# Four transformer layers on one core: unit loads, weight loads and padding memsets moved across the border between a layer's prologue and its attention

## What is computed

```
x = x + linear_attention(xn)    * silu(moe_ffn(xn))        # layer 0
x = x + relative_attention(xn)  * silu(ternary_ffn(xn))    # layer 1
x = x + rotary_attention(xn)    * silu(grouped_ffn(xn))    # layer 2
x = x + biased_attention(xn)    * silu(clamped_ffn(xn))    # layer 3
```

## Time and profile before

| | |
|---|---|
| median of 3 runs | 2297.72 us (2287.29 to 2298.31) |
| the profiled execution | 2273.22 us, span 2271.4 us, mean granted clock 0.867 |
| PE busy | 1774.4 us (78%) |
| DVE busy | 1304.1 us (57%) |
| ACT busy | 916.0 us (40%) |
| POOL busy | 413.6 us (18%) |
| PE idle before its first matmul of a causal attention | 32.0 us (layer 2), 36.2 us (layer 3) |

### The profile page before, as it was taken

One profiled execution on the slowest core, in us unless ns is written; L12 is line 12 of the kernel. 1 busy time (PEld: TensorE's weight loads), 2 busy tenths in 40 slices (PEclk: granted clock), 3 DMA queues, 4 the chain that ended last, 5 costly groups with the idle time before them and its releaser, 6 DMA issues. The chain is left out here.

```text
span 2271.4 us, 33714 instructions
## 1 busy us (share of the span) xinstructions
PE 1774.4 (78%) x12423; PEld 817.5 (36%) x12423; DVE 1304.1 (57%) x2569; ACT 916.0 (40%) x1719; POOL 413.6 (18%) x340
## 2 busy tenths in 40 slices
PE   5895999537888888888463898885973998969998
PEld 4633444313343333333232343342431444333333
DVE  3224444648466766582433987515464977327888
ACT  1111222414565666566232366651220666532221
POOL 0000000266466756562003000000001000000000
PEclk7787999758999999899786799987985999779999
DMA  4100000356567666562005001000024011000000
GB/s 127 44 19 1 0 0 0 108 160 168 138 147 176 154 160 163 143 168 59 10 23 156 12 21 30 16 1 0 0 65 124 17 30 30 2 1 1 0 0 19
DMA packets 190782, 141.38 MB, mean 62 GB/s; under 512 B 56697, under 2 KB 169513, under 8 KB 190506
## 3 DMA queue, kind: packets, MB, share of 16 engines
q1 hardware_dynamic: 184010, 127.35, 22.0%
q10 hardware_dynamic: 6624, 12.06, 1.7%
HBM read 78.75 MB, written 59.90 MB: 61 GB/s over the span
## 5 line engine op out<-in xcount | busy, mean ns | idle before, releaser
L1628 DVE TENSOR_REDUCE a1a_partial<-a1a_room 128x4 f32<-128x1024 f32 x192 | 225.9, 1220 | 47.5 <-PE a1a_room L1693 46.8
L1590 ACT ACTIVATE a1a_probsT<-a1a_st 128x512 f32<-128x512 f32 (+1 forms) x416 | 204.9, 578 | 54.0 <-PE a1a_st L1726 53.8
L2016 ACT ACTIVATE a3a_probsT<-a3a_st 128x512 f32<-128x512 f32 (+2 forms) x320 | 155.7, 561 | 120.7 <-PE a3a_st L2078 83.8
L2016 ACT ACTIVATE a2a_probsT<-a2a_st 128x512 f32<-128x512 f32 (+2 forms) x320 | 155.7, 561 | 114.7 <-PE a2a_st L2078 79.4
L1936 DVE TENSOR_REDUCE a3a_maxima<-a3a_room 128x2 f32<-128x1024 f32 (+3 forms) x160 | 167.6, 1110 | 53.5 <-PE a3a_room L2050 49.2
L1936 DVE TENSOR_REDUCE a2a_maxima<-a2a_room 128x2 f32<-128x1024 f32 (+3 forms) x160 | 167.6, 1110 | 44.5 <-PE a2a_room L2050 39.7
L745 DVE TENSOR_TENSOR f_mid<-f_b,f_act 128x512 f32<-128x512 f32 x96 | 66.4, 691 | 158.6 <-ACT f_act L707 158.6
L1763 PE MATMUL a1a_ctx<-a1a_probsT,a1a_vpad 128*9 128x512 f32 (+3 forms) x1408 | 150.5, 528 | 0.8
L1496 POOL TENSOR_TENSOR a1a_shifted<-a1a_shifted,a1a_best 128x1024 f32<-128x1024 f32 x64 | 121.8, 1903 | 145.5 <-DVE a1a_best L1634 145.5
L707 ACT ACTIVATE f_act<-f_a 128x512 f32<-128x512 f32 x100 | 59.7, 597 | 203.6 <-PE f_g L678 195.6
L1693 PE MATMUL a1a_room<-stack 48*128 48x128 bf16 (+1 forms) x1376 | 113.3, 266 | 34.4 <-DVE a1a_partial L1628 14.6
(11 more groups left out here) (467 smaller groups left out, 3434.5 us busy)
## 6 DMA issues: line engine op xcount, KB each, us to landing
a1a_band<-a_band SPq DMA_DIRECT2D x112, 192.0 KB, 3.7
a_near<-a1a_shifted SPq DMA_DIRECT2D x112, 192.0 KB, 2.9
a1a_near<-a_near SPq DMA_DIRECT2D x64, 256.0 KB, 4.0
a_band<-a1a_r_mix SPq DMA_DIRECT2D x64, 254.0 KB, 3.4
stack<-q SPq DMA_DIRECT2D x32, 192.0 KB
stack<-q SPq DMA_DIRECT2D x32, 96.0 KB
stack<-k SPq DMA_DIRECT2D x32, 96.0 KB
q<-a1j_parts ACTq DMA_DIRECT2D x10, 256.0 KB, 3.0
```

Of the source, the lines that this page charges most:

```text
L1590: nc.scalar.activation(dst, src, ACT.Exp).then_inc(exp_done, 1)
L1628: nc.vector.tensor_reduce(partial[:, g % 2, :, 1 + r].rearrange("p (a s) -> p a s", a=2), src, X_AXIS, ALU.max).then_inc(job_free, 1)
L2016: nc.scalar.activation(probsT[:, block_at % BLOCK_ROOMS, place:place + heads, lo:], src, ACT.Exp).then_inc(exp_done, 1)
```

## The change

In layers 2 and 3 the prologue's SyncE list now ends after the stores: only unit 0 is loaded there. The loads of units 1 and 2 and those of the FFN's weights stand at the head of SyncE's list in the attention, each unit behind a wait for its batch's stores. The parts of batch 1 live in tiles that outlast the prologue (`last_parts`), so it no longer waits for their stores. `vpad` and its memsets move to the start of GpSimd's list in the prologue (`PaddedValues.fill`), and PE's wait for them is gone. In layer 1 the prologue still waits for the stores of batch 1, but unit 1 is loaded in the attention, after the third band load; the five whole memsets on GpSimd are replaced by four on DVE that write only the corners which no DMA writes. In all three prologues `loads` is split: PE waits for the first 1 or 4 of them, DVE later for the rest.

```diff
@@ near_attention
+            if n == BAND_AHEAD - 1:
+                dma_order += [("load", U) for U in range(1, SETS)]
...
-                for i in range(BANDS + 2):
-                    nc.gpsimd.memset(band[i][:], 0.0).then_inc(pads_filled, 1)
-                pool.wait_ge(pads_filled, BANDS + 2)
...
-                            sp.wait_ge(pads_filled, BANDS + 2)
+                            sp.wait_ge(corners_filled, 4)
...
                 nc.vector.memset(ctx[:], 0.0).then_inc(ctx_zeroed, 1)
+                for lines, i, n, columns_ in ((slice(0, HALF_ROWS), 0, BANDS + 2, slice(WINDOW, NEAR)), (slice(HALF_ROWS, P), 0, BANDS + 2, slice(0, HALF_ROWS)),
+                                              (slice(0, HALF_ROWS), BANDS, 1, slice(0, REACH)), (slice(HALF_ROWS, P), BANDS + 1, 1, slice(NEAR - REACH, NEAR))):
+                    nc.vector.memset(bands[lines, i:i + n, :, columns_], 0.0).then_inc(corners_filled, 1)
@@ PaddedValues
+    def fill(self, pool):
+        for tile in self.tiles:
+            self.nc.gpsimd.memset(tile[:], 0.0).then_inc(self.filled, 1)
+        pool.wait_ge(self.filled, BATCH)
+        for tile in self.tiles:
+            self.nc.gpsimd.memset(tile[:, :, :, DH:DH + 1], 1.0).then_inc(self.filled, 1)
+        pool.wait_ge(self.filled, 2 * BATCH)
@@ causal_attention
-                for b in range(BATCH):
-                    nc.gpsimd.memset(vpad[b][:], 0.0).then_inc(pads_filled, 1)
...
+                for U in range(1, len(stack)):
+                    sp.wait_ge(stored[U % BATCH], 16 * (len(queries.stored) + len(keys.stored)))
+                    load_unit(U)
+                for pairs, sem in after:
+                    start_loads(sp, pairs, sem)
...
-                pe.wait_ge(pads_filled, 2 * BATCH)
@@ prologue
+        if last_parts is not None:
+            parts.append(last_parts)
...
-        LANDED = 16 * len(loads)
+        LANDED, REST_LANDED = 16 * plan.first, 16 * (len(loads) - plan.first)
...
-                    sp.wait_ge(stored[b], 16 * PARTS_STORED)
-                    for U in range(b, len(stack), BATCH):
+                    if b == 0:
+                        sp.wait_ge(stored[b], 16 * stores_of(plan.items))
                         for s, (stacks, _, _) in enumerate(plan.items):
-                            stacks.load(sp, stack[U][s], U // BATCH, b, stacked[U])
-                for pairs, sem in after:
-                    start_loads(sp, pairs, sem)
+                            stacks.load(sp, stack[0][s], 0, 0, stacked[0])
+                if last_parts is None:
+                    sp.wait_ge(stored[BATCH - 1], 16 * stores_of(plan.items))
                 sp.wait_ge(landed, LANDED)
+                sp.wait_ge(rest_landed, REST_LANDED)
...
-                dve.wait_ge(landed, LANDED)
+                dve.wait_ge(rest_landed, REST_LANDED)
...
+                if plan.fills is not None:
+                    plan.fills(pool)
```

More of the change, by code:

```diff
@@ L1443, in near_attention @@
         ctxT, inv = ph.sb("ctxT", [P, 2, CHUNK]), ph.sb("inv", [P, HT, HG])
-        band = [ph.sb(f"band{i}", [P, HG, NEAR]) for i in range(BANDS + 2)]
+        bands = ph.sb("bands", [P, BANDS + 2, HG, NEAR])
+        band = [bands[:, i] for i in range(BANDS + 2)]
         near = [ph.sb(f"near{i}", [P, HG, P]) for i in range(SLOT)]
@@ L1776, in _, with __init__, causal_attention @@
                         mm.then_inc(pv_done, 1)
-def causal_attention(nc, k, tag, queries, keys, values, stack, stacked):
+class PaddedValues:
+    def __init__(self, nc, ph):
+        self.nc = nc
+        self.tiles = [ph.sb(f"vpad{b}", [P, TILES, HG, 32]) for b in range(BATCH)]
+        self.filled = ph.sem("pads_filled")
+    def fill(self, pool):
[5 more added lines that the diff above has]
+        pool.wait_ge(self.filled, 2 * BATCH)
+def causal_attention(nc, k, tag, queries, keys, values, vpad, stack, stacked, stored, after):
     UNITS = BATCH * GROUPS
@@ L1905, in causal_attention @@
     with phase(nc, tag) as ph:
-        vpad = [ph.sb(f"vpad{b}", [P, TILES, HG, 32]) for b in range(BATCH)]
         probsT = ph.sb("probsT", [P, BLOCK_ROOMS, HG, CHUNK])
@@ L2109, with stores_of, prologue @@
     crossed_at: int = 0
-def prologue(nc, k, tag, loads, plan, stack, stacked, after):
+    first: int = 1
+    fills: object = None
+def stores_of(items):
+    return sum(len(stacks.stored) for stacks, _, _ in items)
+def prologue(nc, k, tag, loads, plan, stack, stacked, stored, last_parts=None):
     N, J, HALF_T = len(plan.items), len(plan.jobs), NT // BATCH
     per_batch = {eng: 2 * sum(job[3] == eng for job in plan.jobs) for eng in ("dve", "act")}
-    PARTS_STORED = sum(len(stacks.stored) for stacks, _, _ in plan.items)
     def seen(engine, b, j, x):
@@ L2153, in _ @@
             def _(sp):
-                start_loads(sp, loads, landed)
+                start_loads(sp, loads[:plan.first], landed)
+                start_loads(sp, loads[plan.first:], rest_landed)
                 for b in range(BATCH):
@@ L2416, in biased_attention @@
         values = ph.sb("values", [P, NT, DIM])
-        stack = causal_sets(k)
-        stacked = [ph.sem(f"stacked{n}") for n in range(len(stack))]
+        stack, vpad = causal_sets(k), PaddedValues(nc, ph)
+        stacked, stored = [ph.sem(f"stacked{n}") for n in range(len(stack))], [ph.sem(f"stored{b}") for b in range(BATCH)]
+        last_parts = [ph.sb(f"last_parts{i}", [P, 3, SEQ], BF16) for i in range(2)]
         with phase(nc, "a3p") as pw:
@@ L2623, in relative_attention @@
                         tops={0: [(0, 0)], 1: [(0, 1), (0, 2)]}, rests={1: [(0, 0)], 2: [(0, 1), (0, 2)]}, middles={1: [(0, 0)], 2: [(0, 1), (0, 2)]},
-                        wide=wide, unfold=unfold, unfolded=2)
-            prologue(nc, k, "a1j", loads, plan, stack, stacked, after)
+                        wide=wide, unfold=unfold, unfolded=2, first=4)
+            prologue(nc, k, "a1j", loads, plan, stack, stacked, stored)
         near_attention(nc, k, "a1a", queries, [lefts, rights], [left_values, right_values], stack, stacked, rel)
@@ L2760, in layer @@
                 elif n == 1:
[L2761 removed]
+                    attention(nc, k, part("attn"), attn_tiles)
                 else:
```

37 lines of the change are left out of this document (16 added, 21 removed).

## The result

The changed kernel took 2230.9 us (median of 4 executions, 2225.3 to 2236.6), the kernel before 2298.0 us beside it (2287.3 to 2300.1): 67 us less by the two medians (2230.9 / 2298.0 = 0.971). The estimated ratio, which isn't the quotient of the two medians, is 0.9744 with a 95% interval of 0.9705 to 0.9783: 59 us less, from 50 to 68. The forecast was 51 us and a time of 2246.6 us; its range of 2233 to 2261 misses the median by 2 us on the low side and holds what the ratio gives (0.9744 x 2297.7 = 2239). The two profiled executions differ by less than the medians: 2273.2 us before (clock 0.867), 2225.3 us after (clock 0.876), 48 us. Of all executions of a kernel in one session, those more than 1.5% above its fastest are left out of medians and ratios here, which takes out 3 of the kernel before and none of the others.

The account below looks back on a forecast made before the run. Before each attention engines waited for SyncE, which waited for stores and issued loads nobody needed yet. Layers 2, 3 and 1 gave 17.6 + 23.2 + 10.3 = 51.1 us, subtracted from the median 2297.7: 2246.6 us, range 2233 to 2261.

Parts of the forecast that it names:

- The direction and the mechanism: Borders of prologue and attention: SyncE arrives last, in layers 2 and 3 no engine computes for 13 and 20 us; faster 0.94.
- Layer 2: Border of prologue and attention: 16.3 us from PE's earlier start plus 1.3 from splitting loads, 17.6 together, from 15.5 to 18.3.
- the split of `loads`: Layer 2's prologue: PE no longer waits for `l_sin` to turn the weights; at least 0.76 us, at most 2.0, taken 1.3.
- Layer 3: Border of prologue and attention: PE starts at 1709.8 instead of 1733.0, gain 23.2 us, from 21.0 to 24.2.
- rival (a): Barriers of layers 2 and 3: unit 0 isn't there yet; 2 and 3 us less gain, 44 in all, 2254 us; 14%.
- Layer 1: Start of attention: first `r_mix` 10.8 us earlier, less 0.5 for tile 3's band; gain 10.3 us, from 7.5 to 10.8.
- The corner memsets: Layer 1, four on DVE: 2.7 us of work, a price of 2.7 us if they held up `r_mix`, taken as 0.
- The band of tile 3: Layer 1: its load, behind unit 1's, is just in time; 0.5 us taken off, between nothing and 2.5.
- What would show it: Trace signs: PE's wait ends within 1 us of the barrier, DVE doesn't wait for tile 3's band, later stretches last as before.
- The slacks: Late loads aren't missed: 14 us for unit 1 and 9 for rows of maxima in layer 2, 4 in layer 3.
- rival (c): Shorter pauses lower the clock throughout the attentions; outweighs 51 us from 5.4%, at 8% a loss of 77 us, 2323; 3%.
- 57 us or more: Case of a gain of some 57 us or more, if PE also keeps the full clock at the attention's start; 5%.

Follow-up runs that it names:

- weights_early: Changed kernel with the weights' loads of layers 2 and 3 issued in the prologue again, ahead of SyncE's last waits: 2253.4 us, ratio 0.9826.
- vpad_late: Changed kernel with the padded values of layers 2 and 3 filled behind the barrier again, with PE's wait for them: 2239.2 us, ratio 0.9779.
- l1_unit1_later: Changed kernel with layer 1's unit 1 loaded behind band 3's load instead of ahead of it: 2237.9 us, ratio 0.9752.
- layer1_undone: Changed kernel with unit 1 of layer 1 loaded in the prologue again and GpSimd zeroing the bands: 2252.7 us, ratio 0.982.
- l2_delay: Changed kernel with 19 memsets of an unused tile on DVE ahead of layer 2's first maxima: 2244.1 us, ratio 0.9784.
- weights_first: Changed kernel with late loads of layers 2 and 3 in opposite order (FFN weights, unit 2, unit 1): 2232.8 us, ratio 0.9735.
- l1_delay: Changed kernel with 19 memsets of an unused tile on GpSimd at the start of layer 1's attention: 2245.6 us, ratio 0.9796.
- pe_filler: Changed kernel with 24 unread 128x512 matmuls at the end of PE's prologue list in layers 2 and 3: 2246.4 us, ratio 0.9787.

## Why the prediction was right or wrong

**The direction and the mechanism** were right: SyncE was the last to arrive, and behind it stood clears and memsets. `weights_early` shows that by putting one part of the queue back, `vpad_late` by putting the memsets back.

**Layer 2.** Forecast 17.6 us, measured 19.5. The border itself was forecast at 16.3 and measured 16.15. The rest lies between the statistics and the end of GpSimd's last sum, which came 3.1 us sooner; the prediction had taken 1.3, at most 2.0, for the split of `loads`. No run undoes the split alone, but the rows show how it works. PE's first products for queries and keys, before and after:

```profile
1182.63 3.78 PE L2195 MATMUL a2j_bank<-xnT,a2p_wideT 128*128 128x512 f32 x4 [0.68 <-ACT xnT L2238]
...
1171.65 3.47 PE L2223 MATMUL a2j_bank<-xnT,a2p_wideT 128*128 128x512 f32 x4 [0.68 <-ACT xnT L2266]
```

The statistics start at 1173.31 and 1165.26, so the products come 9.3 us behind them before and 6.4 after. DVE's waits in the prologue, before:

```profile
DVE a2p_q L2479 <- PE a2j_bank L2195: 3.3, 4, 1.3
DVE a2p_key L2479 <- PE a2j_bank L2195: 3.1, 2, 2.2
DVE a2p_partner_q L2479 <- PE a2j_bank L2195: 0.9, 4, 0.4
```

And after:

```profile
DVE a2p_key L2511 <- PE a2j_bank L2223: 2.3, 2, 2.1
DVE a2p_q L2511 <- PE a2j_bank L2223: 1.5, 2, 1.3
DVE a2p_partner_q L2511 <- PE a2j_bank L2223: 0.5, 3, 0.2
```

In sum 7.3 and 4.3 us (the columns are the total, the number, the longest). The argument counted one wait, of 0.76 us, and a part of the short ones behind it; all those behind it that hung on PE had to be summed. The upper bound was wrong as well as the value. The lower end of the range for this layer, 15.5, and that of layer 1, 7.5, are not worked out in the prediction from its terms (10.8 less 2.5 is 8.3).

**Layer 3.** Forecast 23.2 us, measured 23.3 (60.8 to 37.5) in the two first profiles, 22.2 in the later pair. That PE would wait for unit 0 until about 1 us behind the earliest start was in the sum, and the row shows 0.9 us behind the barrier. It isn't a fixed price: over the eight profiles in which `stack` ends this wait it is from 0.8 to 3.0 us, and the border of 37.5 us becomes 40.0 (`l1_unit1_later`). In that one, in `layer1_undone`, `l2_delay` and `weights_first` SyncE starts unit 0's loads some 5 us behind its store of batch 0's last key part; in the changed kernel it is 3.6 us, 1676.10 to 1679.66. So a part of what those versions lose is rival (a) in layer 3. Why that store takes longer to land in them isn't shown.

**Layer 1.** Forecast 10.3 us, measured 9.5 and 10.3, and 10.3 with this part alone. The corner memsets cost nothing. The band of tile 3 was late by 0.85 us, where 0.5 were taken off; that DVE should not wait for it, as "What would show it" says, didn't hold. At first sight the trace says less: `a1o_acc` starts 7.4 us earlier only. But the 602.1 us of the first profile of before are short for this stretch (602.1 and 607.9 in the kernel before; 600.2 to 607.1 over eight profiles with layer 1 as changed), so no loss behind the border is shown.

**The slacks.** Both units' held in the changed kernel, and `weights_first` issued unit 1 10 and 11 us later still. The place of the late loads was "the tightest" in layer 3 with 4 us; rows of the maxima start at 1712.51 and SyncE is free at 1706.75: 5.8 us.

**What was off** is the last step, from the sum to the time: "The stretches behind should last as long as before", and 51.1 taken off a median of three executions. The borders sum to 52.2 us, 1 us from the forecast. On the profiled execution the same sum gave 2222 us, and 2225.3 were measured. The 15.7 us by which the forecast was above the median come apart so: 5.3 because the 2297.7 of before stood above its 2292.4 over 54 executions; 1.1 from the borders; 0.9 because the changed kernel's first median is below its later one; and some 8 us by which it gains more than its borders. The first is the luck of three executions. The last is inside the intervals, as said. If it is real, the granted clock gives a size. Over the 54 executions of before the span falls by 1.5 us for each 0.001 of mean clock (correlation -0.82); their means are 2291.3 us and 0.8594. Taking out 52 us at 0.50, the clock of the empty stretches, would raise the mean to (2291.3 x 0.8594 - 52 x 0.50) / 2239.3 = 0.8677; the ten executions of the changed kernel have a mean of 0.8714. The 0.0037 that are left are worth about 5 us, an estimate. So most of the 8 us stands in the clock. The prediction's rival (c) asked only if shorter pauses lower the clock; what the clock shows has the other sign. The 5% for "57 us or more" came true in its number and not in its mechanism: it wanted PE to keep the full clock at the attention's start, and the clock is 0.50 there before and after. That the attentions differed by 5 us in one profile was seen, and taken into the range alone.

**What stays open.** Which stage gets the better clock, and why, isn't settled. The attentions of the changed kernel's two profiles (283.3, 277.9, 283.3, 286.5) and of the kernel before's (278.5, 283.6, 291.9, 282.5) overlap; four profiles are too few. What nothing touches varies as well: up to layer 1's statistics the 14 profiles take from 407.2 to 415.6 us, and layer 2's FFN lasts 152.4 to 152.8 us in nine of them and 154.7 to 155.7 in five, `layer1_undone` and `weights_early` among these. Nor is it known in full why `layer1_undone` loses 21 us, when `l1_delay` with the same border loses 14 in the median; the two differ by 1.1 us in PE's wait for unit 0 in layer 3.

## What to carry to other kernels

At a barrier, find the engine that arrives last and read what it did in its last microseconds: issuing a DMA cost the queue's engine from 0.34 us (`l_wg`) over 1.4 (the `w_s`, in the mean) to 5.7 us (`l_bias`), whether or not anyone wanted the data yet, and in layer 2 the 15 issues behind the last store, with a wait for that store, held all engines for 13 us. Keep ahead of it only what is needed at once, and take the slack of the rest from the length of the first work behind it; moved loads delay what stands behind them in their new place in the queue, as the band of tile 3, or of tile 4.

Before a gain is subtracted from a median, look at how far the same code's stretches differ in the trace: where two equal attentions last 278 and 284 us, three executions don't fix a base to within 5 us.

## What the runs showed of the hardware

Attentions of the same instructions last 278 us at a mean granted clock of 0.90 and 291 to 294 at 0.83, with DVE busy for the same 184.4 to 184.9 us. The clock was at 0.50 in the first 30 to 35 us of each of them (in `pe_filler` from some 5 us on), and again for some 10 to 55 of the last 60 us, and it is mainly this last part whose share differs.

A matmul of 128x512 with float32 operands is recorded as two of 0.43 us at full clock, 24 of them as 48 in 20.8 us.

The time that SyncE takes to issue a single DMA differs more than tenfold: in the changed kernel's layer 3, `l_w_up` takes 0.40 us, `l_w_down` 4.33, `l_bias` 5.74 and `l_down_bias` 0.42. For `l_bias` it is 5.71 to 5.76 us in 13 of the 14 profiles and 6.99 in `weights_first`.

A load issued right ahead of the last stores can be the last thing to be ready: PE waited for unit 0 in layer 3 until 0.8 to 3.0 us behind the barrier.

The full clock didn't outlast the filler: after 20 us of matmuls without a gap at 1.00 it was 0.50 again 4 us into an attention in which PE was busy for 0.4 to 0.8 of each microsecond.
